# Causal mask by TensorE products, near mask on GpSimd, in the distance attention of a decoder layer

## The reference

```python
qn = sum(q * q); kn = sum(k * k); qk = q @ k.T            # 16 heads of 8
diff_sq = maximum(qn[:, None] - 2.0 * qk + kn[None, :], 0.0)
ed = sqrt(diff_sq + 1e-8); ns = qn[:, None] + kn[None, :]
dist_taylor   = ed * (1 + c * ns * 0.5 + c * c * ns * ns * 0.125)
dist_asymp    = 0.693 + log(ed + 1e-8) + c * ns * 0.25
dist_standard = ed * sqrt(1 + c * ns)
dist = where(ed < 0.1, dist_taylor, where(ed > 2.0, dist_asymp, dist_standard))
scores = where(causal, -beta * dist, -inf)
o = softmax(scores) @ v
```

## Time and profile before

| | us |
|---|---|
| median of 3 runs | 257.37 |
| lowest, highest | 255.42, 258.94 |
| the profiled execution | 257.91 |
| its span, first to last instruction | 256.1 |
| busy in the span: PE, DVE, ACT, POOL | 198.7, 192.6, 157.2, 111.4 |
[...]

### The profile page before, as it was taken

The page is one execution under the profiler, slowest core; times in us unless marked ns, Lnnn a source line. Parts: engine busy times, 40 slices in busy tenths (PEclk is TensorE's granted clock), DMA queues, the critical chain, the costliest instruction groups (busy, mean ns, idle before and its releaser), DMA issues. The chain is left out here.

```text
span 256.1 us, 6417 instructions
## 1 busy us (share of the span) xinstructions
PE 198.7 (78%) x2340; PEld 151.3 (59%) x2341; DVE 192.6 (75%) x547; ACT 157.2 (61%) x321; POOL 111.4 (44%) x151
## 2 busy tenths in 40 slices
PE   0697352756677767687899885999999898999995
PEld 0263131535455555475656741378888797888884
DVE  5868889997899999996856789664786943656554
ACT  2499879994999998873364221475555559342320
POOL 9730355674465544627144035002367754734000
PEclk9999955555898777755589778699999999999999
DMA  4305575884187059300001200000000000100001
GB/s 120 89 1 138 147 184 141 220 210 101 42 240 219 15 146 344 97 3 0 3 4 65 102 0 0 0 3 0 0 1 4 0 3 0 41 1 3 0 4 41
DMA packets 28396, 17.49 MB, mean 68 GB/s; under 512 B 11588, under 2 KB 26444, under 8 KB 28108
## 3 DMA queue, kind: packets, MB, share of 16 engines
q1 hardware_dynamic: 28364, 17.08, 24.1%
HBM read 12.09 MB, written 4.98 MB: 67 GB/s over the span
## 5 line engine op out<-in xcount | busy, mean ns | idle before, releaser
L1313 DVE SCALAR_TENSOR_TENSOR dist_mem<-P,gub,dist_mem 128x512 f32<-128x512 f32 x32 | 23.8, 749 | 24.4 <-ACT dist_mem L873 23.9
L873 ACT ACTIVATE dist_mem<-P,gub 128x512 f32<-128x512 f32 x32 | 21.9, 688 | 30.7 <-PE P L1352 30.7
L607 POOL TENSOR_SCALAR m_gt<-dist_mem 128x640 uint8<-128x640 f32 x16 | 29.2, 1825 | 6.7 <-issue 4.8
L1352 PEld LDWEIGHTS PO<-proj_mem,dist_mem 128*128 128x128 f32 x244 | 29.4, 192 | 1.0
L1352 PE MATMUL PO<-proj_mem,dist_mem 128*128 128x128 f32 x244 | 30.0, 276 | 0.0
L1352 PE MATMUL P<-cf,dist 128*128 128x128 f32 x80 | 22.5, 365 | 6.7 <-ACT shift L801 6.7
L1352 PE MATMUL P<-xhi,whi 128*128 128x512 f32 x64 | 26.6, 415 | 1.1 <-DVE dist_mem L1313 1.1
L596 POOL TENSOR_TENSOR dist<-dist,cf 128x128 f32<-128x128 f32 x16 | 7.3, 457 | 45.1 <-DVE dist L1071 45.1
L1352 PE MATMUL P<-xhi,wlo 128*128 128x512 f32 x64 | 25.0, 391 | 0.0
L1352 PE MATMUL P<-xlo,whi 128*128 128x512 f32 x64 | 25.0, 390 | 0.0
L1352 PEld LDWEIGHTS P<-cf,dist 128*128 128x128 f32 x80 | 14.7, 184 | 12.2 <-ACT shift L801 9.7
(11 more groups left out here) (255 smaller groups left out, 527.8 us busy)
## 6 DMA issues: line engine op xcount, KB each, us to landing
q_split<-split_mem SPq DMA_DIRECT2D x16, 128.0 KB, 2.5
k_split<-split_mem SPq DMA_DIRECT2D x4, 512.0 KB, 3.7
stq<-q_split SPq DMA_DIRECT2D x16, 128.0 KB
stk<-k_split SPq DMA_DIRECT2D x16, 128.0 KB
split_mem<-no_rows SPq DMA_DIRECT2D x1, 1024.0 KB, 5.1
wgu<-gate_w SPq DMA_DIRECT2D x1, 1024.0 KB, 5.7
wgu<-up_w SPq DMA_DIRECT2D x1, 1024.0 KB, 10.0
dist<-no_rows SPq DMA_DIRECT2D x1, 1024.0 KB, 5.0
```

The lines of the kernel that those rows point to most:

```text
L607: pool.tensor_scalar(m_gt[:, g.k % 2, :], e2[:, g.k % 2, :], 4.0 - ATT_EPS, None, ALU.is_gt).then_inc(sm["gt_done"], 1)
L873: A(sil[:, f, :], (P1, P2)[f][:, 0, :], ACT.Silu, bias=gub[:, 0, one:one + 1]).then_inc(sm["sil_done"], 1)
L1313: V.scalar_tensor_tensor(hT[:, z % 2 * 2 + f, :], (P1, P2)[f][:, 1, :], gub[:, 1, one:one + 1], sil[:, f, :], ALU.add, ALU.mult).then_inc( ...
L1352: return nc.tensor.matmul(out_, lhsT, rhs, start=start, stop=stop, **more)
```

## The change

The constant that masks keys ahead of the query moves into the score products. TensorE adds, behind the four products of each strip, four products of the identity's first 32 columns with a bf16 constant of 32 columns, for both heads (64 columns): 1024 is added to the squared distance in P1 and 2^32 to the norms in P2, where the key lies ahead. Through the far branch such a score becomes so large that its exponential is 0. GpSimd's three additions per unit and their semaphore are left out; the minima wait for `dist_done`. m_ge is made by GpSimd from e2 (e2 >= 0.01 - 1e-8), ahead of m_gt, and no longer by VectorE. The fp32 constants shrink by 64 columns, the bf16 ones grow by 64. Nothing else moves.

```diff
@@ gpsimd, step
-                g = s - 1
-                if g.there():
-                    wait(pool, "dist_done", g.n(1))
-                    row = dist[:, g.k % 4, :]
-                    cm = cf[:, C_CM:C_CM + ST]
-                    cm2 = cm.unsqueeze(1).broadcast_to([128, 2, ST])
-                    ends = row[:, 256:512].rearrange("p (j n) -> p j n", j=2)[:, :, 64:128].rearrange("p j (q n) -> p j q n", q=2)
-                    pool.tensor_tensor(ends, ends, cm.unsqueeze(1).unsqueeze(1).broadcast_to([128, 2, 2, ST]), ALU.add)
-                    for strip in (3, 1):
-                        end = strip_of(row, strip)[:, :, strip * ST:(strip + 1) * ST]
-                        last = pool.tensor_tensor(end, end, cm2, ALU.add)
-                    last.then_inc(sm["causal_done"], 1)
                 g = s + 1
                 if g.there():
                     wait(pool, "e2_done", g.n(1))
+                    wait(pool, "sel_done", g.n(-1))
+                    pass_waits(pool)
+                    pool.tensor_scalar(m_ge[:, g.k % 2, :], e2[:, g.k % 2, :], 0.01 - ATT_EPS, None,
+                                       ALU.is_ge).then_inc(sm["ge_done"], 1)
                     wait(pool, "dist_done", g.n(-1))
@@ vector, step
-                    wait(dve, "causal_done", low.n(1))
+                    wait(dve, "dist_done", low.n(1))
...
-                if near.there():
-                    wait(dve, "e2_done", near.n(1))
-                    wait(dve, "sel_done", near.n(-1))
-                    V.tensor_scalar(m_ge[:, near.k % 2, :], e2[:, near.k % 2, :], ATT_EPS, 0.01, ALU.add,
-                                    ALU.is_ge).then_inc(sm["ge_done"], 1)
@@ tensor, scores
+                far = B_CAUSAL + (ST if P is P2f else 0)
+                causal = cb[:, far:far + ST].unsqueeze(1).broadcast_to([128, 2, ST])
                 for strip in (3, 2, 1, 0):
                     for g in range(4):
                         q = sq_[k][:, g, bl * S + strip * ST:bl * S + (strip + 1) * ST]
                         keys = right[k][:, g * PB + bl, :, 0:(strip + 1) * ST]
-                        last = mm(strip_of(P[g * ST:(g + 1) * ST, :], strip), q, keys)
+                        mm(strip_of(P[g * ST:(g + 1) * ST, :], strip), q, keys, stop=False)
+                    for g in range(4):
+                        ends = strip_of(P[g * ST:(g + 1) * ST, :], strip)[:, :, strip * ST:(strip + 1) * ST]
+                        last = mm(ends, ident_b[:, 0:ST], causal, start=False)
                 last.then_inc(sm[done], 1)
```

More of the change, by code:

```diff
@@ L69 @@
 FAR = 1e30
+FAR_KEY, FAR_NORM = float(2 ** 10), float(2 ** 32)
 C_ID = 0
 C_BLK = 128
-C_CM = 256
-C_NSEL = 320
+C_NSEL = 256
 C_COL = C_NSEL
@@ L88 @@
 B_NSEL = B_HEAD + XH
-B_TOT = B_NSEL + CB
+B_CAUSAL = B_NSEL + CB
+B_TOT = B_CAUSAL + 2 * ST
 BLOCKS = (((3, 0, 128),), ((3, 1, 128),), ((2, 0, 96), (0, 0, 32)), ((2, 1, 96), (0, 1, 32)), ((1, 0, 64), (1, 1, 64)))
@@ L117, in constants @@
     c[:, C_BLK:C_BLK + 128] = same(p // 32) & same(p % 4)
-    c[:, C_CM:C_CM + ST] = np.where(np.arange(ST)[None, :] > (p % ST)[:, None], FAR, 0.0)
     col = c[:, C_COL:C_COL + 16]
@@ L150, in constants @@
         b[:, B_NSEL + n] = -1.0 * ((p % 32 < CB * XH) & (p % 32 // XH == n))
+    for n, far in enumerate((FAR_KEY, FAR_NORM)):
+        b[0:ST, B_CAUSAL + n * ST:B_CAUSAL + (n + 1) * ST] = np.where(p[None, :ST] > p[:ST, None], far, 0.0)
     tri = np.triu(np.ones((S, S), np.float32))
@@ L319, in decoder_layer @@
                  "shift_done oT_done ge_done da_done sel_done prod_done dist_done nm_done o_copied o_done "
-                 "x1_done gt_done causal_done nmT_full t_full pv_done oT_full wo_full g_full pre_done l1p_done "
+                 "x1_done gt_done nmT_full t_full pv_done oT_full wo_full g_full pre_done l1p_done "
                  "lf_done cs_full aT_done ar_full rm_done rx_done rt_full em_done enm_done ex_full dT_done cT_done hs_done hr_done lg_full "
@@ L994, in step @@
                 k_ = s.k
-                low, far, near = s - 2, s - 1, s + 1
+                low, far = s - 2, s - 1
                 t = s - 4
```

## The result

| | before | after |
|---|---|---|
| median, us | 257.12 | 260.42 |
| lowest, highest | 255.42, 258.94 | 258.74, 263.16 |
| the profiled execution's span | 256.1 | 258.3 |
| mean granted TensorE clock | 0.833 | 0.872 |
| code fetches on the instruction queue (16 KB each) | 19 | 23 |

The ratio is 1.0125, 95% interval [1.0063, 1.0187]: slower by 3.3 us where the sum said 0.4 faster. The time lies within the predicted range, the direction doesn't agree. A ratio leaves out the slow executions of a kernel, those over 1.5% above its fastest (here 263.16), so it can differ from the quotient of the medians, which count all of them; where that changes a reading, both are given.

What follows compares the result with a forecast made beforehand. VectorE and ScalarE, both nearly full, were taken to bound the causal attention. The terms -3.2 + 0.6 + 0.9 + 0.2 + 1.5 - 0.4 gave -0.4 us, so 257.0 us from a median of 257.37; range 252.5 to 261.5.

Steps and rivals of the forecast that it cites:

- Unit 6 stayed with the SP queue: Attention near 59.4 us: unit 6 is due by SP's transfers, so up to some 4 us won or lost earlier is absorbed.
- `prod` is caught at the edge: VectorE's step: m_ge on GpSimd blocks until T + 2.41, just when prod starts; taken as 0, 0.33 per step kept for range.
- m_ge, -3.2: VectorE's steps 6 to 14: dropping m_ge wins 0.41 us in five and 0.29 in four, 3.2 us.
- Mask products on TensorE: Score groups: added products run side by side; +0.6 us in the refill, +0.9 in low-clock steps, +0.2 at unit 15's norms.
- What a free GpSimd triggers: Attention's end: centring and weight splits move to about 119.5 to 124.5 us and block VectorE, +1.5 (0 to 3), relief -0.4.
- The relief of 0.4: At 134 to 138 us, GpSimd work moved earlier removes 0.44 us of TensorE idling: -0.4 us.
- GpSimd's additions go, worth 0: GpSimd's queue in the attention: dropping 1.10 us of additions per unit, hidden since the minimum comes later, gains 0.
- B: Rival: the gain stays whole and busier TensorE gets the high clock more often; 253.6 us, chance 0.27.
- C: Rival: GpSimd's m_ge catches prod in every step; 260 to 262 us, chance 0.12; extreme form 268, chance 0.03.
- D: Rival: mask products don't run side by side, 264 us, or early GpSimd work costs 3, 258.5 us; chance 0.08.

Runs made afterwards that it cites:

- e_pad: Kernel before plus 512 TensorE products of the identity with zeros, placed as the masks are; GpSimd's additions and VectorE's m_ge stay: 260.43 us, ratio 1.0097.
- e_late: Changed kernel, but GpSimd waits for the last unit's dist before it centres the context, as the additions made it do before: 257.72 us, ratio 1.0051.
- e_norm: Changed kernel with the mask in P2 only, 256 of the 512 mask products left out, GpSimd's early work kept: 257.73 us, ratio 1.0053.
- e_one: Changed kernel with one full-width mask product per strip for all four row groups, 128 mask products instead of 512: 276.07 us, ratio 1.0768.
- e_maskonly: Changed kernel with m_ge back on VectorE at its old place; mask by TensorE and additions left out remain: 262.20 us, ratio 1.0199.
- e_one_late: e_one with GpSimd's work held back as in e_late: 273.96 us, ratio 1.0641.
- e_norm_late: Changed kernel with GpSimd's early work held back as in e_late and the mask in P2 only, 256 mask products: 254.58 us, ratio 0.9854.
- e_geonly2: Kernel before, additions kept and no masks on TensorE, with m_ge on GpSimd behind m_gt and one unit further ahead: 257.59 us, ratio 0.9996.
- e_padN: Kernel before plus 256 TensorE products of the identity with zeros, in the norms' group in P2 only: 257.16 us, ratio 0.9979.
- e_padK: Kernel before plus 256 TensorE products of the identity with zeros, in the squared distance's group in P1 only: 257.68 us, ratio 1.0006.
- e_pad_shift: e_pad with 96 small idle TensorE products ahead of the attention, which shift all later code: 261.47 us, ratio 1.0147.
- e_move: e_late with the three transfers of zeros and context (2 MB) issued one stack later: 257.51 us, ratio 0.9967.

## Why the prediction was wrong, and where it was right

**Right.** Unit 6 stayed with the SP queue (its key products start at 59.7, 59.36 in the earlier trace rows). m_ge takes 1.81 us on GpSimd and is ready in time. Four of the steps without a stop take 4.85 to 4.90 us, as forecast, a fifth 5.28. The mask products run side by side at their lower bound, 0.11 us more per group at the high clock. The 1.2 and 2.4 GHz beside that bound are in no row; the earlier trace rows have 640 columns in 0.53 us, 1.2 per ns, at the low clock and in 0.28, 2.3 per ns, at the high one. `prod` is caught at the edge, 0.82 to 0.96 us (+0.5 in eight steps): m_ge starts at T + 1.95, 0.12 later than worked out. Unit 6 restarts 1.0 us late where the sum had 0.6.

**Where the 3.6 us between sum and result lie.** The range held, and that is little merit: three terms were off in the same direction. Products: 1.7 in the sum, 2.5 measured (`e_pad`). Early GpSimd work less its relief: 1.1, and 2.6 (or 1.9 by `e_late`). m_ge: -3.2, and -1.9. That makes 0.8 + 1.5 + 1.3. None of the three differences is clear of its own interval; that the sum is on the wrong side is.

**m_ge, -3.2: about right in the steps, less in the time.** By the runs it is -1.9, uncertain by 2.4. The sum took the 0.41 and 0.29 for all nine steps; two of them (8 and 12) ended with a stop of TensorE, and in those VectorE's gain only lengthens its wait.

**The step that failed first: "Mask products on TensorE", +0.6 + 0.9 + 0.2.** As a size it was near: 1.7 against 2.5, uncertain by 1.0, by e_pad. As a mechanism it was not complete. The 0.9 stood for steps at the low clock. In the profile of after they hardly came, the clock being 1.00 from 70 to 100 us; in that of e_pad one did, with x_sb waiting 0.88 us at 76.24 behind products at the low clock and no stop. The code that the products bring was put at nothing, without a reason. 512 products and their 512 loads fill 4 fetches of 16 KB, and behind some fetches TensorE stops: 1.9, 2.4 and 1.6 us in the kernel after. VectorE's waits for x_sb are 3.4 us there against 0.6 before, 4.4 in e_pad. The row for it was at hand: the stop at 100.8 us before, in a stretch with every DMA engine busy, which I passed over since VectorE didn't wait for it.

**The step that failed second: "What a free GpSimd triggers", +1.5 - 0.4.** The first price was near, 1.8 us at one place where the sum had 1.5: T of 15 to D of 14 is +1.8 in after, in e_norm and in e_one (8.9) and +2.1 in e_maskonly (9.2), and +0.0 to 0.4 in every kernel in which that work is held back or the additions stand before it. It came 2 us later than worked out, since the block copies didn't move forward: they follow m_gt, which waits for VectorE's select with or without the additions. So it met other operations too: of the 1.8, 1.1 is the one `nm`, 0.4 a gate product (`gf`) and 0.3 `runmax`, and `prod` wasn't touched. The relief of 0.4 isn't to be seen: the next unit takes 6.2 us as before, and over all kernels 5.4 to 6.2 with no order in it. By the ratios the whole is 1.9 us (e_late; 0 to 3.8), 3.3 (e_one_late; 0.9 to 5.7) and 5.1 (e_norm_late; 3.5 to 6.7). The rows have 1.8 at this place in all three pairs; what the last has beyond that is open, and the profiles show 2.6 us of span there.

**"GpSimd's additions go, worth 0."** Wrong as an independent term: without it the move of m_ge is +19 us at this place of the queue, and 0 at the other. Two edits that were costed apart depend on each other through one queue.

**The rivals.** B's clock came in the profiled execution of after, not in its others, and B's time didn't; the time is the one that C gave, 260 to 262, but C's block is only 0.5 us in the kernel after, so C would have been right by luck; the block takes the whole gain only in e_geonly2; D's condition (not side by side) didn't occur, though the time that it stood for, a TensorE that stands in the way, did in part.

**Open.** Why the products' cost isn't in proportion. What the rows show is where stops land: ahead of the out-projection or inside it, VectorE pays most of their length; inside the product with V it pays little. With all 512 products a long stop (1.5 to 1.9 us) landed just ahead of unit 8's out-projection in after, e_pad and e_late, with half of them inside the product with V in e_padN, e_padK, e_norm and e_norm_late. e_maskonly meets the same instruction with a stop of 0.5 us only, and is none the faster. The total of e_pad_shift speaks against place, its stretches behind unit 6 for it. That TensorE has too little free time left to make good a stop once all products are in would fit e_pad too, and no run here isolates it. Open as well is what decides whether a fetch brings a stop.

## What to carry to other kernels

An instruction added to an engine's straight-line code can be paid twice: in its own time and in code that has to be fetched. Count the added instructions in fetches (here 512 products and their 512 loads brought four, 23 against 19), look in the trace of before for stops whose "issue" row waits for nothing, and ask what stands right behind them and who waits for it. When work leaves an engine's in-order queue, cost what moves forward in that queue as an edit of its own; here one wait that held it back gave back about half of the loss. Before two edits are costed apart, write the queue of each engine with only one of them in it. And halve a change before dropping it: with half of its products and the held-back queue this one turns from 1.25% slower into 1.5% faster (1.0% with the transfers moved as well).

## What the hardware showed unexpectedly

- A stop of TensorE behind a code fetch: from the packet's start to TensorE's next product 2.4 us in after (78.2 to 80.6, and 99.8 to 102.15) and 2.4 in before (100.4 to 102.85), each amid transfers that take over 90% of the DMA engines' time. It is not shorter where they are few: 2.6 us in after at 105.8 to 108.4 and in `e_move` at 107.5 to 110.1, both at 7%. Busy DMA engines alone don't bring a stop either: fetches at 78.4 in before (95% from 77 to 80 us) and at 82.0 in after brought none.
- In `e_one` changing between products of 32 columns and of full width costs about 0.12 us per change at the low clock (0.50), 0.94 us in a group of 20 with its eight changes.
- GpSimd's comparison to 8 bits (TENSOR_SCALAR) holds up a two-input VectorE operation only in its first 0.6 us (0.58 by the earlier trace rows; 0.7 to 0.8 in `e_geonly2`, where it is itself delayed by 0.14 to 0.25); its subtraction (TENSOR_TENSOR) held one to its end in after (`nm` 1.24 us, ended at 128.3 with it) and was itself held, 2.76 us in place of 1.26.
- A step without a stop takes as long at either level of TensorE's clock: that of unit 9 takes 4.89 us in after with 1.00 granted and 4.90 in `e_late` with 0.50. VectorE and ScalarE are the bound of those steps. And a busier TensorE isn't always granted more: `e_one` has it busy 9.3 of 10 us at 0.50.
